# Values of batches 5 to 7 moved behind attention steps 14 to 24, with w2's load behind them

## The reference, cut to what matters

```python
# layer 0, cross attention with 16 heads of 64
xn = layernorm(layernorm(x)) * gamma + beta
q  = xn @ w_q                       # 128 -> 1024
k, v = split(ctx @ w_kv)            # 128 -> 1024 each
out = softmax(q k^T / 8) v @ w_out + b_out
x = x + tanh(g) * tanh(gate) * out
# layer 0, experts: top 2 of 8, w1 128 -> 256, relu, w2 256 -> 128
# layer 1, one-head cross attention, then shared + top 2 of 8 experts,
#          We1 128 -> 512, silu, We2 512 -> 128
```

## Time and profile before

| | |
|---|---|
| median of three runs | 302.24 us |
| profiled execution | 301.93 us |
| its span, first to last instruction | 300.2 us |
| TensorE busy | 277.2 us, 92% |
| VectorE busy | 192.3 us, 64% |
| ScalarE busy | 166.6 us, 55% |
| GpSimd busy | 96.3 us, 32% |
| mean granted TensorE clock | 0.998 |

### The profile page before, as it was taken

One profiled execution on the slowest core, in us unless ns is written; L12 is line 12 of the kernel. 1 busy time (PEld: TensorE's weight loads), 2 busy tenths in 40 slices (PEclk: granted clock), 3 DMA queues, 4 the chain that ended last, 5 costly groups with the idle time before them and its releaser, 6 DMA issues.

```text
span 300.2 us, 6266 instructions
## 1 busy us (share of the span) xinstructions
PE 277.2 (92%) x2157; PEld 238.4 (79%) x2157; DVE 192.3 (64%) x607; ACT 166.6 (55%) x354; POOL 96.3 (32%) x144
## 2 busy tenths in 40 slices
PE   1999997899989978999998999999899999999995
PEld 0477875688878866888986898788779889999985
DVE  2797968488899988246758577635967722432106
ACT  2494349878867756332355553668626631566560
POOL 1167006468855542012016531100101430155610
PEclk9999999999999999999999999999999999999999
DMA  7692100099600000090000000000000245921122
GB/s 183 205 305 31 3 0 3 0 263 244 136 3 2 1 2 0 5 314 3 0 2 0 0 3 0 1 2 0 2 1 2 76 137 189 276 94 40 42 87 71
DMA packets 20526, 20.49 MB, mean 68 GB/s; under 512 B 2097, under 2 KB 15049, under 8 KB 20496
## 3 DMA queue, kind: packets, MB, share of 16 engines
q1 hardware_dynamic: 19088, 18.09, 21.2%
q0 software_dynamic: 1120, 1.88, 2.8%
q10 hardware_dynamic: 288, 0.13, 0.2%
HBM read 15.86 MB, written 4.24 MB: 67 GB/s over the span
## 4 chain that ended last, share of the span: by engine, by line
PE 65%; DVE 19%; POOL 5%; issue 4%; ACT 3%; DMA 2%; SPq 0%; DVEq 0%; ACTq 0%; POOLq 0%
PE bank L1252 10%; PE bank L1431 9%; PE bank L1225 7%; PE bank L1226 6%; PE bank L1227 6%; PE bank L1419 4%; PE bank L1412 4%; DVE xhat_sb L908 4%; PE bank L1210 4%; POOL p_sb L643 3%; DVE sum_sb L845 3%; PE bank L1170 3%; DMA ctx_tok_sb<-in_ctx 2%; PE bank L1181 2%; DVE negmax_sb L834 2%
## 5 line engine op out<-in xcount | busy, mean ns | idle before, releaser
L786 ACT ACTIVATE hT_sb<-bank,cols_sb 128x512 f32<-128x512 f32 x72 | 48.6, 689 | 52.8 <-PE bank L1227 52.4
L643 POOL TENSOR_TENSOR p_sb<-p_sb,recip_sb 128x480 f32<-128x480 f32 x32 | 31.6, 989 | 48.1 <-DVE recip_sb L848 48.1
L1147 DVE SCALAR_TENSOR_TENSOR x_sb<-bank,wts_sb,x_sb 128x128 f32<-128x128 f32 x96 | 27.0, 343 | 26.1 <-PE bank L1431 17.2
L1252 PEld LDWEIGHTS bank<-we_sb,hT_sb 128*128 128x128 f32 x320 | 37.1, 192 | 1.2 <-issue 0.5
L1252 PE MATMUL bank<-we_sb,hT_sb 128*128 128x128 f32 x320 | 38.0, 276 | 0.0
L695 POOL TENSOR_TENSOR rstd_sb<-veps_sb,minus_half_sb 128x4 f32<-128x4 f32 (+1 forms) x11 | 11.0, 999 | 66.9 <-DVE veps_sb L900 66.6
L1431 PE MATMUL bank<-w_sb,hT_sb 128*128 128x128 f32 x256 | 31.5, 276 | 0.0
L1431 PEld LDWEIGHTS bank<-w_sb,hT_sb 128*128 128x128 f32 x256 | 30.4, 192 | 1.2 <-issue 0.4
L796 ACT ACTIVATE p_sb<-bank,bias_t_sb 128x128 f32<-128x128 f32 x60 | 17.1, 371 | 16.3 <-PE bank L1412 16.3
L1181 PE MATMUL bank<-ident_sb,p_sb 128*120 128x128 f32 x128 | 19.7, 280 | 4.9 <-POOL p_sb L643 4.6
L686 POOL DMA_INDIRECT ys_hbm<-w_kv_sb,targets_sb x15 | 14.4, 960 | 25.9 <-DVE w_kv_sb L817 25.6
(11 more groups left out here) (217 smaller groups left out, 609.0 us busy)
## 6 DMA issues: line engine op xcount, KB each, us to landing
xs_hbm<-col_rows_sb SPq DMA_DIRECT2D x1, 2145.0 KB, 15.8
we_sb<-in_L_ffn_We SPq DMA_DIRECT2D x1, 2048.0 KB, 9.0
w_sb<-in_L_ffn_We SPq DMA_DIRECT2D x8, 256.0 KB, 3.1
w_after_sb<-in_L_ffn_We SPq DMA_DIRECT2D x7, 256.0 KB, 3.9
w_kv_sb<-in_L_xattn_w_kv SPq DMA_DIRECT2D x2, 512.0 KB, 6.9
w_sb<-in_L_ffn_w SPq DMA_DIRECT2D x1, 1024.0 KB, 11.0
w_kv_sb<-xs_hbm SPq DMA_DIRECT2D x15, 65.0 KB, 2.9
x_sb<-in_x SPq DMA_DIRECT2D x1, 512.0 KB, 7.4
```

The lines of the kernel that those rows point to most:

```text
L643: nc.gpsimd.tensor_tensor(p0[j % 4], p0[j % 4], recip0[:, j % 2, :].unsqueeze(2) .broadcast_to([128, HG, SK]), ALU.mult).then_inc(probs_re ...
L786: nc.scalar.activation(hT[:, u % 2, c, :], ps(item)[:, :], ACT.Relu if n == 1 else ACT.Silu, bias=cols[:, col:col + 1]).then_inc(read(item ...
L1147: last = nc.vector.scalar_tensor_tensor(out=x[:, b, :], in0=ps(key)[:, C * i:C * (i + 1)], scalar=w, in1=x[:, b, :], op0=ALU.mult, op1=ALU ...
L1252: last = nc.tensor.matmul(ps(key)[:, C * i:C * (i + 1)], hT[:, unit_at[(n, p, e)] % 2, c, 128 * i:128 * (i + 1)], we2[:, e, c, :], start=( ...
```

## The change: where the values, their operands and w2 go

The six items ("v0", 5, 0) to ("v0", 7, 1) leave their place ahead of the keys. One each follows the attention steps 14, 16, 18, 20, 22 and 24, ahead of the w1 split or statistics that stand there. Inside the attention v0 takes the spares 4 and 6 in turn, as q0 does. As six fills leave ahead and the turns go modulo six and two, all other banks stay.

The parts of ctxT and w_v now have to live until step 24: ctxT's share the room of w2, w_v's lie behind w_q's in the room of we2. So w2 is loaded after the last v0 was computed, ahead of We2; the wait for q0 comes before both.

```diff
-    schedule += [("v0", b, p) for b in range(5, B) for p in range(2)]
+    late_values = [("v0", b, p) for b in range(5, B) for p in range(2)]
...
         schedule.append(("attend", i))
+        if i >= 14 and i % 2 == 0 and late_values:
+            schedule.append(late_values.pop(0))
         if 4 <= i < 4 + 2 * E and i % 2 == 0:
...
-            spare = (4, 6) if item[0] == "q0" else (0, 1) if item[0] == "up" else (6,)
+            spare = (4, 6) if item[0] in ("q0", "v0") else (0, 1) if item[0] == "up" else (6,)
...
-        w2 = sb("w2", [128, E, HC0, C])
         with ExitStack() as turn1:
...
+            ctxT_hi, ctxT_lo = sb1("ctxT_hi", [C, B * SK], F32R), sb1("ctxT_lo", [C, B * SK], F32R)
+        w2 = sb("w2", [128, E, HC0, C])
+        with ExitStack() as turn1:
             w_q_hi, w_q_lo = sb1("w_q_hi", [C, INNER], F32R), sb1("w_q_lo", [C, INNER], F32R)
+            w_v_hi, w_v_lo = sb1("w_v_hi", [C, INNER], F32R), sb1("w_v_lo", [C, INNER], F32R)
...
-        with ExitStack() as turn1:
-            ctxT_hi, ctxT_lo = sb1("ctxT_hi", [C, B * SK], F32R), sb1("ctxT_lo", [C, B * SK], F32R)
...
-            w_v_hi, w_v_lo = sb1("w_v_hi", [C, INNER], F32R), sb1("w_v_lo", [C, INNER], F32R)
...
+            wait_full(sp, ("q0", CH - 1, 1))
+            wait_full(sp, ("v0", B - 1, 1))
             load(w2[:], t["L0_ffn_w2"].rearrange("e (k p) c -> p e k c", p=128), "w2")
-            wait_full(sp, ("q0", CH - 1, 1))
```

## The result

The changed kernel takes 311.85 us (median of six runs, 311.33 to 312.26) where the kernel before takes 302.09: ratio 1.0314, interval 1.0288 to 1.0339. Forecast were 308.0 and at most 310.0. The side was right, the size not: +9.8 us in place of +5.8.

The account below looks back on a forecast made before the run. VectorE's norms were taken to bound the stretch up to 27.49, TensorE the one behind it. 301.93 + 0 + 2.0 (clock) + 3.8 (attention) = 307.7; the median stands 0.3 higher, so 308.0, range 303.9 to 310.0.

Parts of the forecast that it names:

- The gain ahead of the attention: Ahead of the attention: 4.16 us of matmuls leave TensorE, hidden behind VectorE's norms, so the gain is 0.
- The rival that TensorE is the bound ahead: Ahead of the attention: up to 4.16 us come off, giving 299.7; chance 0.05, or 0.06 for no change.
- The clock: Behind TensorE's 4.9 us stop: clock falls, 4 us at half speed lose 2.0 us; bounds 0 and 3.
- the wait ahead of 8.06: At the start: TensorE's 2.84 us wait, cited to show that not each stop can be judged by length alone.
- the rival of a clock that stays: Behind the stop ahead of the keys: the clock does not fall, giving 306.0; chance 0.2.
- The attention: Steps 14 to 24: the six value fills cost +3.8 us; low bound 1.7, high 6.5.
- step 16: In the attention, bank 4: o0 was read before, the fill starts at once, 0.46 is taken up, +0.32.
- a bound of 1.07 per fill: In the attention: if every bank 4 fill also waited for ScalarE as a query does, 9.7 in all.
- Step 18's detour over the split: In the attention: ScalarE's value copy delays w1's last split, rstd and xhat; VectorE 2.7 late, after 1.72.
- The loads: w2 issued after the last value: there by 114 to 116, first reader near 129, cost 0.
- The passing on of the delay: Behind the attention: TensorE is dense to the end, so the delay passes on whole.
- fills that wait in both banks: In the attention, or half speed lasting longer: 310.7 and above; chance 0.1.

Follow-up runs that it names:

- Experiment 7: Changed kernel, but ScalarE copies all keys of chunks 0 to 5 and the transposes of x stand behind chunks 5 and 6: 305.33 us, ratio 1.0094.
- Experiments 3 and 5: Changed kernel, late values also computed ahead of the keys (3): ratio 1.0343; with bank 4 at steps 14, 18, 22, bank 6 otherwise (5): 304.44 us.
- experiment 1: Changed kernel with all six late values in bank 6 instead of banks 6 and 4 in turn: 307.51 us, ratio 1.0182.
- experiment 6: Changed kernel with each value behind the w1 split of its step instead of ahead of it: 310.94 us, ratio 1.0280.
- experiment 4: Changed kernel with the values back ahead of the keys, new places in SBUF and late load of w2 kept: 302.05 us, ratio 1.0009.
- after: The changed kernel itself, six values moved into the attention, against the kernel before: 311.85 us, ratio 1.0314.
- experiment 9: Changed kernel with ScalarE copying keys of chunks 0 to 5, spares swapped (bank 4 at steps 14, 18, 22), w1 split ahead of the value: 299.56 us.
- experiment 10: As experiment 9, but values follow the odd steps 15 to 25, all in bank 6: 302.38 us, ratio 1.0002.
- experiment 11: As experiment 10, but values follow steps 17, 19, 20, 21, 23 and 25: 301.91 us, ratio 0.9986.
- experiment 2: Changed kernel with spares swapped, values in bank 4 at steps 14, 18, 22 and bank 6 at the others: 306.13 us, ratio 1.0150.

## Why the prediction was right and wrong, point by point

**The gain ahead of the attention: right.** It was put at 0, with the seventh key fill at 27.49; it came at 27.31. TensorE stopped 4.85 us for 4.9 foretold. Experiment 7 confirms the reason: with the bank read by ScalarE the 4.2 us become real. The rival that TensorE is the bound ahead is false for the kernel as it was changed and true for that one, which is still 3.1 us slower than before, by its attention.

**The clock: right in mechanism, 0.4 short.** 2.0 were forecast, 2.43 measured; half speed lasted 5.4 us after work began, not 4. Experiments 3 and 5 take the stop away and the loss with it. Two of the readings behind the term were weak. The time from the end of the last matmul to the fall was 2.1 in the earlier trace rows and 3.4 here (22.4 to 25.8), and in experiment 7 the clock fell after a stop of 1.9, so the length of a stop alone does not tell whether it falls. And the earlier trace rows show TensorE's pace at the start, not a clock: the windows of the kernel before print a granted clock of 1.00 there, the first row below, while TensorE's weight loads change from 0.32 to 0.18 us at about 12, the two others.

```profile
10.00:12.00 2.00, 2.00 (x3) 0.74 (x3) 1.93 (x9) 0.59 (x1) 0.00 (x0) 1.00 0.54 161
```

```profile
11.48 0.32 PEld L1276 LDWEIGHTS bank<-w_kv_sb,ctxT_sb 128*120 128x120 f32 x1 [0.53 <-issue]
12.22 0.18 PEld L1276 LDWEIGHTS bank<-w_kv_sb,ctxT_sb 128*120 128x120 f32 x1 [0.41 <-issue]
```

The pace is that of half speed, so the term's size had a fair source; what the record of the clock leaves out at the start is open. It also means that the wait ahead of 8.06, which the rival of a clock that stays was built on, was followed by half pace and did not speak for that rival.

**The attention: the step that failed.** The forecast had +3.8 and was 2.8 short. Its step 16 says of bank 4 that o0 was read before the value is written, which is right, and goes no further: it never asked who next writes bank 4. That is o0, one step on, behind ScalarE's copy. The text counted the waits that a fill has ahead of it and not those that it makes for the next user of its bank. It named ScalarE in a bound of 1.07 per fill, and put that away because a query fill stands between the odd steps there. The rest of the term was right: experiment 1, which has the waits of bank 6 and none of bank 4, follows the forecast within 0.2 us up to the scores of step 24. It is 0.6 above it at step 26 and ends at 3.80; that this is the 3.8 of the forecast is in part luck. With the two terms as measured, the sum would have been 301.9 + 2.4 + 6.6 = 310.9 and the median 311.2; the 0.6 up to the measured 311.85 is what the gather took.

**Step 18's detour over the split: right in kind.** It was put at 1.0; experiment 6 shortens the attention by 0.72, with one more wait of o0 changed by 0.3 the other way.

**The loads: right.** Nothing waited for w2; experiment 4 gives 1.0009 for the places in SBUF and the order of the loads.

**The passing on of the delay: nearly.** 0.64 us more came up in the gather behind the attention. It is in the traces of after and of experiments 3 and 5 and in none of the others. GpSimd waited 6.7, 7.8 and 7.8 us in all for its scatters there, but also 6.8 in experiment 6, which has no such loss. What decides it stays open; no run was made on it.

**The range** ended at 310.0 although the text itself had 310.7 for fills that wait in both banks. That case was given 0.1 for a reason that holds for the fill ahead and not for the one behind.

## What to carry to other kernels

When a fill moves into a rotating buffer, ask two questions of each bank: who must have read it before the fill, and who writes it next and must wait for the fill's reader, with everything queued ahead of that reader. Work that was hidden behind another engine's chain gives nothing back when it leaves; the stop that it leaves behind can cost the clock. Between the two engines of a tight pair put extra work behind what the partner waits for: six fills cost 2.0 us there (experiment 9) and 4.3 ahead of the scores (experiment 10), and the most idle time in the old trace was no guide to the place (experiment 11). Step by step only half of the places differed, so this is a rule of thumb from one kernel.

## What the runs showed of the hardware

TensorE's clock fell to 1.2 GHz in the middle of busy work: in experiment 7 at 89.3, 0.9 us after TensorE had resumed from a stop of 1.88, and it stayed there for 3.4 us, 1.6 of them lost. The same stop in the trace of after cost nothing.

The long stop ahead of the keys, 4.8 to 5.0 us, cost 2.43 in after, 2.31 in experiment 1, 1.98 in experiment 2 and 2.53 in experiment 6, by the same matmuls. By the windows the clock was down for 6.8 to 6.9 us in each of the four. What differs is when it fell, 3.4, 3.1, 2.6 and 3.5 us after the last matmul: the earlier in the stop, the more of the low stretch passed while TensorE was idle, and the less work ran slowly (5.4, 5.1, 4.4 and 5.5 us of it). Each matmul of 480 columns took 0.40 us in place of 0.22, so a microsecond of work at the low clock loses 0.45. One trace was kept of each kernel, and its executions differ: in experiment 1 two of four have a mean clock of 0.994 in place of 0.988, and their times, 307.33 and 307.69, are no shorter than those of the others, 307.11 and 307.79. Why is open.

The Trainium skill (TensorE: Matmul & The Clock Gate, section on HAM oscillation) has waits between bursts throttle the engine, and the rows of the long stop agree; it was right to count against the change.
